# A twelve-layer decoder block on one core: four score places, an earlier pair of products, and a last feed-forward taken by groups of four batches

## The reference, cut to what matters

```python
# L0_xattn (16 heads of 16), L1_xattn (8 heads of 64), L2_xattn (16 heads of 16): context of 375 rows x 192
q, k, v = x @ Wq, ctx @ Wk, ctx @ Wv
attn = softmax(clip(q @ k.T * scale, -CLAMP, CLAMP))      # L0 clips, L1 does not, L2 masks instead
x = x + (attn @ v) @ Wo
...
def _L3_ffn_ref(x, w_gate, w_noise, W1, b1, W2, b2):      # 16 experts of 256 -> 512 -> 256
    logits = jnp.zeros((..., E)).at[..., 1].set(100.0)
    top_vals, top_idx = jax.lax.top_k(logits, K)          # K = 4: always experts 0 to 3
    gates_k = jax.nn.softmax(top_vals, axis=-1)
    h = jax.nn.relu(einsum('bsd,edh->ebsh', x, W1) + b1)
    y = einsum('ebsh,eho->ebso', h, W2) + b2
    out = einsum('ebso,bse->bso', y, gates)
```

## Time and profile before

| | us |
|---|---|
| median of 3 runs | 3099.77 |
| the profiled execution | 3105.24 |
| its span | 3103.5 |
| TensorE busy | 2613.3 (84%) |
| VectorE busy | 1446.2 (47%) |
| ScalarE busy | 1289.6 (42%) |
| GpSimd busy | 890.6 (29%) |

### The profile page before, as it was taken

How to read it: one execution, slowest core, us unless ns; L and a number is a source line. 1 busy time by engine, 2 the same in 40 slices (tenths; PEclk the granted TensorE clock), 3 DMA queues, 4 the chain that set the end, 5 groups by cost and what they waited for, 6 DMA issues and landing times. The chain is left out here.

```text
span 3103.5 us, 56465 instructions
## 1 busy us (share of the span) xinstructions
PE 2613.3 (84%) x18499; PEld 1924.0 (62%) x18500; DVE 1446.2 (47%) x3474; ACT 1289.6 (42%) x3858; POOL 890.6 (29%) x572
## 2 busy tenths in 40 slices
PE   5746899879777988998599877999959996989899
PEld 2345666656455555666489734666649995866566
DVE  5685888850544234444522376566550004654211
ACT  1334677742443123333223222677724342862211
POOL 3254455520001022222133244455522222430000
PEclk8867899979898999999899987999979998989899
DMA  2000000000142010000357600000045553013100
GB/s 104 1 1 27 20 16 20 15 30 1 40 107 66 0 44 16 20 15 15 124 192 238 211 33 33 21 20 19 11 186 186 180 184 100 1 43 89 40 14 24
DMA packets 108484, 194.45 MB, mean 63 GB/s; under 512 B 56276, under 2 KB 81060, under 8 KB 96596
## 3 DMA queue, kind: packets, MB, share of 16 engines
q1 hardware_dynamic: 93986, 166.93, 16.8%
q0 software_dynamic: 6816, 18.62, 2.0%
q10 hardware_dynamic: 7570, 7.47, 0.8%
HBM read 174.29 MB, written 18.71 MB: 62 GB/s over the span
## 5 line engine op out<-in xcount | busy, mean ns | idle before, releaser
L1353 POOL TENSOR_TENSOR L_xattn_p<-L_xattn_p,L_xattn_ri 112x1500 f32<-112x1500 f32 (+1 forms) x192 | 435.9, 2270 | 586.6 <-DVE L_xattn_ri L1661 586.6
L1566 ACT ACTIVATE L_xattn_pT<-ps 125x448 f32<-125x448 f32 (+1 forms) x576 | 255.8, 478 | 356.7 <-PE ps L1457 356.5
L1457 PEld LDWEIGHTS ps<-ident,L_xattn_p 112*125 112x125 f32 x1920 | 256.0, 191 | 100.5 <-issue 40.5
L1578 ACT ACTIVATE L_xattn_p<-L_xattn_sa,L_xattn_ng 112x375 f32<-112x375 f32 x512 | 305.1, 603 | 18.1 <-DVE L_xattn_ng L1677 10.4
L1457 PE MATMUL ps<-ident,L_xattn_p 112*125 112x112 f32 x1920 | 292.2, 284 | 9.5 <-POOL L_xattn_p L1353 4.9
L1009 PEld LDWEIGHTS ps<-L_ffn_xsT,L_ffn_w 128*128 128x128 f32 x2240 | 263.7, 194 | 7.0 <-issue 1.9
L1009 PE MATMUL ps<-L_ffn_xsT,L_ffn_w 128*128 128x128 f32 x2240 | 264.7, 277 | 2.4 <-ACT L_ffn_xsT L1039 2.4
L276 POOL TENSOR_TENSOR ln_rstd<-ln_tmp,half 112x8 f32<-112x8 f32 x26 | 44.3, 1719 | 701.2 <-DVE ln_tmp L225 525.1
L1479 PE MATMUL ps<-L_xattn_kT,L_xattn_qm 32*112 32x375 f32 (+1 forms) x1280 | 173.3, 523 | 70.1 <-DVE L_xattn_v L1604 21.4
L1071 DVE TENSOR_TENSOR L_ffn_y<-ps,L_ffn_pack 128x256 f32<-128x256 f32 x70 | 29.7, 425 | 364.6 <-PE ps L1018 364.6
L1018 PE MATMUL ps<-L_ffn_weights,L_ffn_hT 128*128 x840 | 193.5, 380 | 2.3 <-DVE L_ffn_hT L1083 2.3
(11 more groups left out here) (410 smaller groups left out, 5083.4 us busy)
## 6 DMA issues: line engine op xcount, KB each, us to landing
L_ffn_w<-in_L_ffn_experts SPq DMA_DIRECT2D x74, 1024.0 KB, 5.5
L_xattn_src<-in_ctx SPq DMA_DIRECT2D x48, 375.0 KB, 3.0
L_attn_toeplitz<-L_attn_h SPq DMA_DIRECT2D x4, 3136.0 KB, 23.1
L_ffn_weights<-in_L_ffn_experts SPq DMA_DIRECT2D x8, 1028.0 KB, 16.8
L_xattn_keys<-in_ctx SPq DMA_DIRECT2D x16, 281.2 KB, 6.0
L_xattn_rows<-in_ctx_rows SPq DMA_DIRECT2D x16, 281.2 KB
L_ffn_weights<-in_L_ffn_experts SPq DMA_DIRECT2D x8, 516.0 KB, 9.5
L_ffn_w<-in_L_ffn_experts SPq DMA_DIRECT2D x4, 1026.0 KB, 5.9
```

The costliest lines, as they stand in the source:

```text
L1353: g.tensor_tensor(P[:, m % 4, :, :], P[:, m % 4, :, :], ri[:, m % 4, :].unsqueeze(2).broadcast_to([T, W, S2]), ALU.mult).then_inc(s["prob_ ...
L1457: last = pe.transpose(turned(t)[:, j * T:(j + 1) * T], P[:, m % 4, j, kc * KW:(kc + 1) * KW], k.ident[0:T, 0:T])
L1566: act.activation(PT[:, m % 4, kc, :, :].rearrange("p h t -> p (h t)"), turned(t), ACT.Copy).then_inc(s["pt_ev_a"].sem, 1)
L1578: last = act.activation(P[:, m % 4, j, :], at, ACT.Exp, bias=ng[:, m % 4, j:j + 1], scale=-1.0 if mask else 1.0, accum_out=rs[:, m % 4, j: ...
```

## The change

**In L0 and L2** `sa` has four places, so a clamp or a mask step has to wait for the exponentials of step n-4 only. In L0 VectorE's reciprocal of step n-2 moves from ahead of the clamp to behind it, and the maxima are split: first half, then the store of a job (in p0 and p1), then the second half. In L2 the reciprocal moves between the two halves of the maxima, and a copy of one column (`pace`) carries the wait for the place.

**In L1** TensorE's `close_pair` moves from behind the transposes to right behind `open_pair`, ahead of `weigh`.

**The last feed-forward** is new code, `joint_experts`. All four experts' weights are loaded at the start, each into its own slot. The loop goes by groups of four batches, and inside a group over 4 experts x 4 hidden pieces: 64 steps. The gate goes into the activation as its scale, and the first bias is multiplied with it beforehand. The second product is turned: weights are 128 x 128 pieces of `W2`, the moving side is the activation of 448 columns, and it sums over all experts in two PSUM banks. VectorE lifts the sum out with the second bias added, TensorE transposes it back, VectorE adds it to `X`. TensorE makes the first product of step t ahead of the second of step t-2. `fixed_gates` and its pass over `X` are gone.

```diff
@@ -686,69 +686,153 @@
 
     lay, dram = packs[name]
     tile, p = pack_tile(k, ctx, name + "_pack", lay)
+    elay, edram = packs[name + "_experts"]
+    if spec["mode"] == "fixed":
+        joint_experts(k, ctx, name, (tile, dram, lay["_total"]), p, elay, edram, spec)
+        return
...
+def joint_experts(k, ctx, name, pack, p, layout, dram, spec):
+    nc, s = k.nc, k.signals
     logits = [0.0, 100.0, 0.0, 0.0]
+    X, M = spec["experts"], spec["hidden"]
+    per_group = X * M
+    steps = G * per_group
+    LAG, RING = 2, 4
...
+    def load_all(sp):
+        for e in range(X):
+            sp.dma_start(slots[e][:, :], dram[e, :, :]).then_inc(w_in[e].sem, 16)
+    layer_norm(k, pack=pack, ahead=load_all)
...
+        def _(pe):
+            def raise_up(t):
+                g, e, m = place(t)
+                if g == 0 and m == 0:
+                    pe.wait_ge(*w_in[e].at(16))
+                pe.wait_ge(*acted.at(t - 1))
+                for c in range(2):
+                    last = pe.matmul(k.ps[:, t % 2, 0:GT], w1[e][:, c, m * KP:(m + 1) * KP],
+                                     k.XT[:, c, g * GT:(g + 1) * GT], start=(c == 0), stop=(c == 1))
+                last.then_inc(up.sem, 1)
+            def bring_down(t):
+                g, e, m = place(t)
+                pe.wait_ge(*acted.at(t + 1))
+                if t % per_group == 0:
+                    pe.wait_ge(*lifted.at(2 * (g - 1)))
+                for half in range(2):
+                    last = pe.matmul(k.ps[:, 4 + 2 * (g % 2) + half, 0:GT], w2[e][:, m, half * KP:(half + 1) * KP],
+                                     hT[:, t % RING, :], start=(t % per_group == 0),
+                                     stop=(t % per_group == per_group - 1))
+                last.then_inc(down.sem, 1)
+            def turn(g, r):
+                pe.wait_ge(*lifted.at(2 * g + 2))
+                pe.wait_ge(*added.at(2 * g + r - 1))
+                for j in range(2):
+                    for half in range(2):
+                        at = (2 * r + j) * T
+                        last = pe.transpose(k.ps[0:T, 2 + r, j * D + half * KP:j * D + (half + 1) * KP],
+                                            oT[:, g % 2, half, at:at + T], k.ident[:, :])
+                last.then_inc(turned.sem, 1)
+            for t in range(steps + LAG):
+                if t < steps:
+                    raise_up(t)
+                if t >= LAG:
+                    bring_down(t - LAG)
+                if t > per_group and t < steps and t % per_group in (LAG + 1, LAG + 3):
+                    turn(t // per_group - 1, (t % per_group - LAG) // 2)
+            for r in range(2):
+                turn(G - 1, r)
...
+            act.wait_ge(*gate_v.at(1))
+            act.activation(gates[:, :], gates[:, :], ACT.Exp).then_inc(gate_a.sem, 1)
+            k.table(act, spec["act"])
+            for t in range(steps):
+                g, e, m = place(t)
+                if g == 0 and m == 0:
+                    act.wait_ge(*gate_v.at(e + 2))
+                act.wait_ge(*up.at(t + 1))
+                act.wait_ge(*down.at(t - RING + 1))
+                act.activation(hT[:, t % RING, :], k.ps[:, t % 2, 0:GT], spec["act"], bias=b1[:, e, m:m + 1],
+                               scale=gates[:, e:e + 1]).then_inc(acted.sem, 1)
...
+            for g in range(G):
+                v.wait_ge(*down.at((g + 1) * per_group))
+                v.wait_ge(*turned.at(2 * (g - 1)))
+                for half in range(2):
+                    v.tensor_scalar(oT[:, g % 2, half, :], k.ps[:, 4 + 2 * (g % 2) + half, 0:GT], b2[:, half:half + 1],
+                                    None, ALU.add).then_inc(lifted.sem, 1)
+                for r in range(2):
+                    x = k.X[:, (g * GB + 2 * r) * D:(g * GB + 2 * r + 2) * D]
+                    v.wait_ge(*turned.at(2 * g + r + 1))
+                    v.tensor_tensor(x, k.ps[0:T, 2 + r, 0:2 * D], x, ALU.add).then_inc(added.sem, 1)
...
@@ -1226,7 +1310,8 @@
     V = sb("v", [KW, 2, KN, HD // R, R + (E - 1) * dh])
     qm = sb("qm", [KP, 2, E, C, T])
     bqs = sb("bqs", [KP, E * C])
-    sa = sb("sa", [T, 2, W, S2]) if copied else None
+    sa = sb("sa", [T, 4, W, S2]) if copied else None
+    pace = sb("pace", [T, 1]) if mask else None
     P = sb("p", [T, 4, W, S2])
     PT = sb("pT", [KW, 4, KN, W, T])
     oT = sb("oT", [KP, 2, C, T])
@@ -1507,14 +1592,14 @@
                 score(i, n)
                 if W == 2:
                     open_pair(i, n)
+                    close_pair(i, n)
                 weigh(i, n - OUT, first, b)
                 if W == 4 and early:
                     open_pair(i, n)
                     close_pair(i, n)
                 turn_over(i, n - TURN, (0, 1), first)
-                if W == 4 and not early:
+                if not early:
                     open_pair(i, n)
-                if W == 2 or not early:
                     close_pair(i, n)
                 ask(i, n)
                 answer(i, n, first)
@@ -1574,7 +1659,7 @@
                         act.wait_ge(*s["pt_mm"].at((i * U + m - 3) * KN))
                     act.wait_ge(*s["max_done"].at((i * U + m) * HALVES + h + 1))
                     for j in range(2 * h, 2 * h + 2):
-                        at = sa[:, m % 2, j, :] if copied else scores(m)[:, j, :]
+                        at = sa[:, m % 4, j, :] if copied else scores(m)[:, j, :]
                         last = act.activation(P[:, m % 4, j, :], at, ACT.Exp, bias=ng[:, m % 4, j:j + 1],
                                               scale=-1.0 if mask else 1.0, accum_out=rs[:, m % 4, j:j + 1])
                     if h == HALVES - 1:
@@ -1666,12 +1751,12 @@
                     return
                 b, u, p = batch_of(i, n)
                 r = n % 4
-                at = sa[:, n % 2, :, :] if clamp else scores(n)
+                at = sa[:, n % 4, :, :] if clamp else scores(n)
                 for h in halves:
                     two = slice(2 * h, 2 * h + 2)
                     if mask:
                         for j in range(2 * h, 2 * h + 2):
-                            last = v.tensor_tensor_reduce(sa[:, n % 2, j, :], at[:, j, :], mb[:, u, :], -1.0, FMAX,
+                            last = v.tensor_tensor_reduce(sa[:, n % 4, j, :], at[:, j, :], mb[:, u, :], -1.0, FMAX,
                                                           ALU.add, ALU.min, ng[:, r, j:j + 1])
                     else:
                         last = v.tensor_reduce(ng[:, r, two], at[:, two, :], AX.X, ALU.max, negate=True)
@@ -1680,25 +1765,33 @@
             def step(i, n, first, last_turn):
                 b, u, p = batch_of(i, n)
                 early = W == 4 and p == jobs[J_V2][3]
-                if not mask:
-                    share(i, n - 1 - LATE, first)
+                if not copied:
+                    share(i, n - 1, first)
                 if n < U:
                     if mask and p == 0:
                         v.wait_ge(*s["mask_done"].at(b + 1))
                     v.wait_ge(*s["sc_mm"].at(i * U + n + 1))
                     if clamp:
-                        v.wait_ge(*s["exp_done"].at(i * U + n - 1))
-                        v.tensor_scalar(sa[:, n % 2, :, :], scores(n), CLAMP, -CLAMP, ALU.min, ALU.max).then_inc(
+                        v.wait_ge(*s["exp_done"].at(i * U + n - 3))
+                        v.tensor_scalar(sa[:, n % 4, :, :], scores(n), CLAMP, -CLAMP, ALU.min, ALU.max).then_inc(
                             s["sc_read"].sem, 1)
-                if mask:
-                    share(i, n - 1 - LATE, first)
+                    elif mask:
+                        v.wait_ge(*s["exp_done"].at(i * U + n - 3))
+                        v.tensor_copy(pace[:, :], k.half[:, 0:1])
+                if clamp:
+                    share(i, n - 2, first)
                 if early:
                     keep(i, n, "KV")
                 if clamp and n < U:
                     v.wait_ge(*s["sc_read"].at(i * U + n + 1))
-                maxima(i, n, range(HALVES))
+                maxima(i, n, (0,))
+                if mask:
+                    share(i, n - 2, first)
+                    maxima(i, n, (1,))
                 if not early:
                     keep(i, n, "KV")
+                if clamp:
+                    maxima(i, n, (1,))
                 keep(i, n, "Q")
                 add(i, n, first)
                 if mask and p == UB // 2 and not (last_turn and n >= UB):
@@ -3634,7 +3727,7 @@
         small = dict(router=in_lanes(w["w_gate"].T), b2=on_rows(w["b2"]))
         experts = [dict(w1=by_rows(w["W1"][e]), w2=by_rows(w["W2"][e]), b1=columns(w["b1"][e])) for e in range(8)]
     else:
-        small = dict(b2=w["b2"][:4])
+        small = dict(b2=np.concatenate([w["b2"][:4, h * KP:(h + 1) * KP].T for h in range(2)], axis=1))
         experts = [dict(w1=by_rows(w["W1"][e]), w2=by_rows(w["W2"][e]), b1=columns(w["b1"][e])) for e in range(4)]
```

105 lines of the change are left out of this document (51 added, 54 removed).

## The result

The changed kernel takes **3066.72 us** (median of four runs, 3066.13 to 3068.3) against 3100.36 us for the kernel before on the same chip (3097.92 to 3105.62): a ratio of 0.989, 95% interval 0.9875 to 0.9905. The forecast was 3060 us, 3036 to 3083. The two profiled executions have spans of 3103.5 and 3066.6 us.

The account below looks back on a forecast made before the run. TensorE was taken to bound all three attention loops and the last feed-forward. Terms -21 - 14 + 6 - 11 = -40 took the profiled 3105.2 to 3065 us; with the median 5.5 lower, 3060 us, 8-in-10 range 3036 to 3083.

Parts of the forecast that it names:

- Last feed-forward, -21 forecast: Last feed-forward: cheaper products, added transposes, earlier start, higher clock and longer tail sum to -21.0 us, bounds -14 and -23.
- Start -9.0: Last feed-forward: first product no longer waits for the bias pass over X, starting at 2878.7 instead of 2887.74, -9.0 us.
- -14.5 + 3.4 - 2.7: Last feed-forward: fewer, wider second products -14.5 us, added transposes +3.4, first round at the higher clock -2.7.
- Tail: End of last feed-forward: lifts, transposes, one more addition and hand-overs take 3.8 us for 2.0, +1.8.
- L0, -14 forecast: L0 loop: two old TensorE waits go, new waits for GpSimd's division come; period 19.85 us, -14, bounds -30 and 0.
- the walk over VectorE and GpSimd: L0: chain from key store through VectorE's work, GpSimd's division, transposes and key job closes the loop at 19.9 us.
- L2, +6 forecast: L2 loop: -0.8 us a batch at p0's scores, +1.1 for the late division, +0.1 at p3's scores; +6, bounds -16, +18.
- L1, -11 forecast: L1 loop: waits for stored jobs go (-2.17 us a batch), two of 0.74 for exponentials come; -11, bounds -35 and 0.
- (1): L0 and L2: divisions stay hidden and both reach TensorE's floor; 3022 us, 12% including cases half way to it.
- (2): Attention loops: gains are eaten by their new waits and only the feed-forward's is left; 3079 us, 17%.
- (3): L0 and L2: every step's transposes wait for the division, reciprocal late in all four steps; +62, 3162 us, 5%.
- (4): L2's p3: the copy pace stands behind GpSimd's whole division through a lock between the engines; +21 us, 3081 us, 6%.

Follow-up runs that it names:

- l0_recip: Changed kernel with L0's reciprocal ahead of the clamp again in the first step of a batch; 3059.51 us, ratio 0.9861.
- places_only: Kernel before with only four score places in L0 and L2 and the clamp's later wait, VectorE's order as before; 3103.47 us in one run.
- l1_swap: Changed kernel with L1's pair the other way round, full-height half opening and half-height half closing; 3077.69 us in one run.
- l2_recip: Changed kernel with L2's reciprocal in step p2 ahead of the store of the second value job again; 3046.37 us, ratio 0.9817.
- l1_turn_first: Changed kernel with L1's exponentials ahead of ScalarE's copies and, in p0 and p2, weigh behind the first two thirds of the transposes; 3039.17 us, ratio 0.9791.
- l1_mid: Changed kernel with weigh between the half-height and full-height halves of L1's pair in p0 and p2; 3063.29 us in one run.
- ffn_alone: Kernel before with the new last feed-forward only; 3079.2 us, ratio 0.9924.

## Why the prediction held, point by point

**Last feed-forward, -21 forecast, -22.3 measured.** Start -9.0 against 18.28 to 8.92, -9.4. First product to last product's end: 209.6 us before (2887.74 to 3090.37 + 6.92), 195.3 now (2863.76 to 3059.07), -14.2 against -14.5 + 3.4 - 2.7 = -13.8; a group of four transposes takes 0.44 us from its start to that of the next products, 0.11 each and not 0.14. Tail 6.2 to 7.5 us, +1.3 against +1.8. The four transfers, now 9.5 us to land, were not waited for. The bounds held.

**L0, -14 forecast, -18.6 by the period.** The mechanism stood: both old waits gone, new short ones in front of the transposes for GpSimd. Mis-sized was the wait in p1, taken as 0.7: the trace has 0.27 there (at 453.13) and 0.28 in p0. That is 0.45 us less waiting than forecast, and 0.27 us of it shows in the period; which piece of the walk over VectorE and GpSimd was too long was not tried. That the wait for the division is what holds the loop is shown by `l0_recip`. The stage fell by 20.5, 1.9 more than the period gives; where these lie was not found. A stage's length can differ by more than that with the same loop: `places_only` has 364.8 us for 367.5 and `l1_swap` 344.4 for 347.0, with the period unchanged in both.

**L2, +6 forecast, +4.6 by the period.** The wait in p3 is 1.0 us (forecast 1.1) and `l2_recip` shows it to be the whole loss and more. Of the two waits for the maxima before, the one in front of p0's scores (0.79 us at 2097.54) is gone as forecast; the one in front of p3's scores was 0.19 us (at 2093.51) and is 0.26 to 0.28, where 0.1 more was forecast.

**L1, -11 forecast, -4.6 by the period.** This is the term that was mis-sized. The two waits for the exponentials are as forecast (2.28 us from turn to pair). What the sum lacked is TensorE's own time: it took each part of the pair at its duration in the old order. In p0 and p2, with the half-height half ahead of it and `weigh` behind, the full-height half takes 1.91 us start to start for 1.73 (values, 512 columns) and 1.46 for 1.28 (keys): 0.36 us. In p1 and p3 it takes 0.97 for 0.87 (256 columns) and 1.36 for 1.28, but the transposes behind it take 0.42 for 0.52, which gives that back; there the half-height half, now behind the wait, takes 0.63 for 0.53 and 0.83 for 0.73, and in `l1_turn_first`, without the wait, 0.53 and 0.73 again. That is 0.56 us a batch in all. The two old waits were worth 2.30 us start to start, not 2.17. So 22.70 - 2.30 + 1.48 + 0.56 = 22.44, and 22.42 was measured. `l1_mid` takes back the term of p0 and p2 (-0.36, less the wait that returned: -0.30), `l1_swap` adds changes of height (+0.78). To take each group at its old duration was wrong once its neighbours had another height.

**The sum and the rest.** Stages -43.0 against -40. That these lie so close is luck: by the stages' lengths L0 gave 6.5 us more than forecast and L1 6.3 less. The nine stages that the diff does not touch took 6.1 us more in this execution, which no step had. Part of it comes back in every kernel with the new L2 loop: the two stages behind L2 together take 500.1 to 502.5 us in these nine kernels and 497.3 to 497.8 in the five with the old loop. Why stays open. The rest is within what these stages show where their code is the same: the nine add up to between 1770.7 and 1775.7 us in the five and to between 1774.3 and 1782.7 us in the nine.

A stage's length also hangs on the granted clock at its start. The L2 stage of the old loop took 344.27 us before and 341.89 in `ffn_alone`; the difference lies between the norm and the first division, 24.85 us at a granted clock of 0.69 and 22.45 at 0.79. The new loop, with its period at 20.04 in all seven kernels that have it, took 348.7 us in the changed kernel and 352.0 to 352.1 in five of the others. So the table's +4.4 for L2 is the low end of +4.4 to +7.9. Last, the profiled execution was taken to lie 5.5 us above the median; the new one lies 1.6 above. The untouched stages (+6.1) and this (+3.9) pushed the time up by 10.0 us, and the four stages took 3.0 of them back. But for rounding, that leaves the 6.7 us by which 3060 was too low.

**The rivals.** (1), divisions hidden, 3022 us: not so here, but with the reciprocal moved in one step L2 comes to 18.89 us a batch (`l2_recip`) and L0 to 19.12 (`l0_recip`), 0.1 and 0.3 us above TensorE's busy time. (2), attention's gains eaten: no; by the periods attention gives 18.6 us in L0 and 4.6 in L1, and loses 4.6 in L2. (3) did not come: the division is late in one step of L2, by 1.0 us, and in two of L0, by 0.3. (4), `pace` against GpSimd: this row sums up all 64 copies.

```profile
L1780 DVE COPY L_xattn_pace<-half x64: 139/154/155, 1921.8 to 2231.3; 112x1 f32<-112x1 f32 x64
```

17 of them start while a division is running, and the longest of all took 155 ns. So here a copy of one column was not blocked by GpSimd, and the lock that the prediction cites did not show on it. Whether such a copy falls under that rule at all, no run here tells.
